# First stage of a two-layer graph and mixture-of-experts kernel on one core: two GpSimd roots of different groups in one instruction, eight scatters in a row behind it

## The reference

```python
x = x + gnn0(_layernorm(x), adj)        # adj @ (x @ w) + b
x = x + ffn0(_layernorm(x))             # attention over 64 nodes, then 8 experts, 2 per token
x = x + gnn1(_layernorm(x), adj)
x = x + ffn1(_layernorm(x))             # 6 experts, 2 per token
...
def _rmsnorm(v, w):
    return v * rsqrt(mean(v * v) + 1e-6) * w
# inside ffn0:
h = _rmsnorm(x, ln1_w)
...
x = x + y @ wo.T                        # y: softmax attention
flat = _rmsnorm(x, ln2_w)
probs = softmax(flat @ router_w.T)      # the two largest of 8 choose the experts
```

## Time and profile before

| what | us |
|---|---|
| time, median of 3 runs | 855.92 |
| the three runs | 860.66, 855.92, 854.97 |
| the profiled execution | 854.43 |
| its span, first to last instruction | 852.5 |
| busy PE / PEld / DVE / ACT / POOL | 811.2 / 624.2 / 697.4 / 521.3 / 426.0 |

### The profile page before, as it was taken

One profiled execution on the slowest core, in us unless ns is written; L12 is line 12 of the kernel. 1 busy time (PEld: TensorE's weight loads), 2 busy tenths in 40 slices (PEclk: granted clock), 3 DMA queues, 4 the chain that ended last, 5 costly groups with the idle time before them and its releaser, 6 DMA issues.

```text
span 852.5 us, 21598 instructions
## 1 busy us (share of the span) xinstructions
PE 811.2 (95%) x6244; PEld 624.2 (73%) x6245; DVE 697.4 (82%) x2699; ACT 521.3 (61%) x1120; POOL 426.0 (50%) x413
## 2 busy tenths in 40 slices
PE   7998999999788899999999999899999999999997
PEld 7675777777547899999999999566665655555563
DVE  4899988989867798877777888888888888888863
ACT  3666787786645466556565654556566656655664
POOL 4248888888877300940100042566665566666300
PEclk9899999999999999999999999999999999999999
DMA  9602411131115766676666762344443344443323
GB/s 269 178 12 78 114 52 48 54 112 42 45 42 171 201 189 174 172 194 167 174 170 163 176 181 75 111 123 124 122 124 120 118 138 147 152 131 121 108 88 99
DMA packets 107591, 108.25 MB, mean 127 GB/s; under 512 B 27822, under 2 KB 89600, under 8 KB 105344
## 3 DMA queue, kind: packets, MB, share of 16 engines
q1 hardware_dynamic: 96976, 88.52, 36.4%
q0 software_dynamic: 8880, 18.19, 7.0%
q10 hardware_dynamic: 1664, 0.66, 0.3%
HBM read 82.07 MB, written 25.26 MB: 126 GB/s over the span
## 4 chain that ended last, share of the span: by engine, by line
PE 61%; issue 4%; POOL 3%; DVE 1%; DMA 1%; ACT 0%; SPq 0%; POOLq 0%; DVEq 0%
PE banks L2073 16%; PE banks L2113 10%; PE banks L2237 10%; PE banks L2229 9%; PE banks L2205 7%; PE banks L2088 2%; PE banks L2134 2%; PE banks L2145 1%; PE banks L2162 1%; PE banks L2251 1%; PE banks L2174 1%; POOL slots_in L1292 1%; POOL expert_rows L1352 1%; PE banks L2154 1%; DMA slots_out<-ys 0%
## 5 line engine op out<-in xcount | busy, mean ns | idle before, releaser
L1352 POOL DMA_INDIRECT expert_rows<-slots_out,slot_c x128 | 140.8, 1100 | 74.6 <-DVE ys L1610 42.1
L326 POOL DMA_INDIRECT slots_in<-flat,slot_now x115 | 120.7, 1050 | 35.7 <-issue 31.2
L2073 PE MATMUL banks<-xT_hi,w_hi 128*128 128x256 f32 (+1 forms) x426 | 127.0, 298 | 0.4 <-DVE w_lo L1629 0.4
L2073 PE MATMUL banks<-xT_hi,w_lo 128*128 128x256 f32 (+1 forms) x426 | 120.7, 283 | 0.0
L2073 PE MATMUL banks<-xT_lo,w_hi 128*128 128x256 f32 (+1 forms) x426 | 120.4, 283 | 0.0
L2113 PE MATMUL banks<-w_sb,prod 128*128 (+1 forms) x852 | 107.1, 275 | 2.4 <-DVE ys L1610 2.4
L2113 PEld LDWEIGHTS banks<-w_sb,prod 128*128 128x128 f32 (+1 forms) x852 | 101.3, 191 | 2.8 <-issue 2.6
L2073 PEld LDWEIGHTS banks<-xT_hi,w_hi 128*128 128x128 f32 (+1 forms) x426 | 76.2, 179 | 0.6 <-issue 0.6
L2073 PEld LDWEIGHTS banks<-xT_lo,w_hi 128*128 128x128 f32 (+1 forms) x426 | 76.6, 180 | 0.0
L2073 PEld LDWEIGHTS banks<-xT_hi,w_lo 128*128 128x128 f32 (+1 forms) x426 | 76.2, 179 | 0.0
L1426 ACT ACTIVATE w_hi<-w_raw 128x684 fp32r<-128x684 f32 x71 | 54.9, 773 | 26.3 <-PE banks L2073 26.3
(11 more groups left out here) (306 smaller groups left out, 2116.7 us busy)
## 6 DMA issues: line engine op xcount, KB each, us to landing
w_raw<-in_w SPq DMA_DIRECT2D x71, 342.0 KB, 3.4
f_all<-gates_dram SPq DMA_DIRECT2D x16, 1024.0 KB, 6.7
xs<-slots_in SPq DMA_DIRECT2D x71, 128.0 KB, 2.6
slots_out<-ys SPq DMA_DIRECT2D x71, 128.0 KB
f_all<-gates_dram SPq DMA_DIRECT2D x16, 512.0 KB, 4.5
base_all<-in_x SPq DMA_DIRECT2D x16, 256.0 KB, 4.2
out<-ob SPq DMA_DIRECT2D x16, 256.0 KB
slots_in<-zrow SPq DMA_DIRECT2D x20, 128.0 KB, 3.5
```

Of the source, the lines that this page charges most:

```text
L326: G.indirect_dma_start(out=slots_in, out_offset=bass.IndirectOffsetOnAxis(ap=slot_now0[g % 2][:, n:n + 1], axis=0), in_=flat[g % 2][:, n / ...
L1352: G.indirect_dma_start(out=rows[p][:, n, :], out_offset=None, in_=slots_out[0:filled(g) * R, :], in_offset=bass.IndirectOffsetOnAxis(ap=sl ...
L2073: last = T.matmul(banks[bank][0:m, half * R:(half + 1) * R], ww[:, par, n * HIDP + c * P:n * HIDP + c * P + m], xx[:, par, :], start=q == ...
```

## The change

For the groups 0 to 11 (`g < JOINT`, with `APART = 4`) the root of the sum of squares is no longer an instruction of its own. VectorE writes the mean of squares of group g as a third row of `var_b` beside the variances of group g + 4, and GpSimd's `rstd1(g + 4)` takes all three rows in one instruction of 128 x 12. It waits for both. The groups 12 to 15 keep their own root. The joint root and the eight scatters of a round now stand together: the root behind `ln_pow`, then 5, 1, 7 of one group and 0, 3, 6, 4, 2 of the next. On ScalarE `flat_` of these groups moves from behind `xn_` to a place between `exp` and `hp_` of its next round. On VectorE `var1` goes ahead of `yn_`. The pipeline gets one more (empty) round.

```diff
+            APART, JOINT = 4, NG - 4
-            var_b, rs_b = sb("var_b", [P, NG, 2, TG]), sb("rs_b", [P, NG, 2, TG])
+            var_b, rs_b = sb("var_b", [P, NG + APART, 3, TG]), sb("rs_b", [P, NG + APART, 3, TG])
...
-            DEEP = 7
+            DEEP = 8
...
                     def rstd1(g):
                         if g is not None:
+                            n = 2
                             pool.wait_ge(at["var1"], upto("var1", g + 1))
-                            G.tensor_tensor(rs_b[:, g, :, :], var_b[:, g, :, :], mhalf[:, 0:2 * TG].rearrange("p (k t) -> p k t", k=2), ALU.pow).then_inc(at["rstd1"], 1)
+                            if exists(g - APART):
+                                n = 3
+                                pool.wait_ge(at["ssv"], upto("ssv", g - APART + 1))
+                            G.tensor_tensor(rs_b[:, g, 0:n, :], var_b[:, g, 0:n, :], mhalf[:, 0:n * TG].rearrange("p (k t) -> p k t", k=n), ALU.pow).then_inc(at["rstd1"], 1)
...
                     def rms(g):
-                        if g is not None:
+                        if g is not None and g >= JOINT:
...
                     def body(g, new):
                         ln_pow(new)
-                        scatter(2, g[6])
+                        rstd1(g[1])
+                        if g[6] is None or g[6] >= JOINT:
+                            scatter(2, g[6])
                         scatter(5, g[6])
                         rms(g[5])
                         scatter(1, g[6])
                         scatter(7, g[6])
                         scatter(0, g[5])
-                        rstd1(g[1])
                         scatter(3, g[5])
                         scatter(6, g[5])
                         scatter(4, g[5])
+                        if g[5] is not None and g[5] < JOINT:
+                            scatter(2, g[5])
...
                     def flat_(g):
...
-                            act.wait_ge(at["rms"], upto("rms", g + 1))
+                            if g < JOINT:
+                                act.wait_ge(at["rstd1"], upto("rstd1", g + APART + 1))
+                            else:
+                                act.wait_ge(at["rms"], upto("rms", g - JOINT + 1))
...
                         exp(g[6])
+                        if g[8] is not None and g[8] < JOINT:
+                            flat_(g[8])
                         hp_(g[4])
...
                         xn_(g[2])
-                        flat_(g[7])
+                        if g[7] is not None and g[7] >= JOINT:
+                            flat_(g[7])
                         vd(g[5])
...
                         slotf(g[6])
                         mv1(g[2])
                         slot(g[6])
+                        var1(g[2])
                         yn_(g[5])
-                        var1(g[2])
```

More of the change, by code:

```diff
@@ L170, in build @@
             st_b, mv_b = sb("st_b", [P, NG * TG, 6]), sb("mv_b", [P, NG * TG, 2])
-            var_b, rs_b = sb("var_b", [P, NG, 2, TG]), sb("rs_b", [P, NG, 2, TG])
+            var_b, rs_b = sb("var_b", [P, NG + APART, 3, TG]), sb("rs_b", [P, NG + APART, 3, TG])
             nmr, inv_h, ratio = (sb(n, [P, NG * TG]) for n in ("nmr", "inv_h", "ratio"))
-            ss, ssv = (sb(n, [P, NG * TG]) for n in ("ss", "ssv"))
+            ss = sb("ss", [P, NG * TG])
             mx, rden = sb("mx", [P, NH, TG]), sb("rden", [P, TG, NH])
@@ L309, in rstd1 @@
                         if g is not None:
+                            n = 2
                             pool.wait_ge(at["var1"], upto("var1", g + 1))
-                            G.tensor_tensor(rs_b[:, g, :, :], var_b[:, g, :, :], mhalf[:, 0:2 * TG].rearrange("p (k t) -> p k t", k=2), ALU.pow).then_inc(at["rstd1"], 1)
+                            if exists(g - APART):
+                                n = 3
+                                pool.wait_ge(at["ssv"], upto("ssv", g - APART + 1))
+                            G.tensor_tensor(rs_b[:, g, 0:n, :], var_b[:, g, 0:n, :], mhalf[:, 0:n * TG].rearrange("p (k t) -> p k t", k=n), ALU.pow).then_inc(at["rstd1"], 1)
                     def rms(g):
-                        if g is not None:
+                        if g is not None and g >= JOINT:
                             pool.wait_ge(at["ssv"], upto("ssv", g + 1))
-                            G.tensor_tensor(tiles(rr2, g), tiles(ssv, g), mhalf[:, 0:TG], ALU.pow).then_inc(at["rms"], 1)
+                            G.tensor_tensor(tiles(rr2, g), var_b[:, g + APART, 2, :], mhalf[:, 0:TG], ALU.pow).then_inc(at["rms"], 1)
                     def scatter(n, g):
@@ L440, in flat_ @@
                                 n = g * TG + t
-                                last = S.activation(flat[g % 2][:, t, :], f2_all[:, n, :], ACT.Copy, scale=rr2[:, n:n + 1])
+                                root = rs_b[:, g + APART, 2, t:t + 1] if g < JOINT else rr2[:, n:n + 1]
+                                last = S.activation(flat[g % 2][:, t, :], f2_all[:, n, :], ACT.Copy, scale=root)
                             last.then_inc(at["flat"], 1)
@@ L632, in ssv_ @@
                             dve.wait_ge(at["ssq"], upto("ssq", g + 1))
-                            V.tensor_scalar(tiles(ssv, g), tiles(ss, g), 1.0 / C, 1e-6, ALU.mult, ALU.add).then_inc(at["ssv"], 1)
+                            V.tensor_scalar(var_b[:, g + APART, 2, :], tiles(ss, g), 1.0 / C, 1e-6, ALU.mult, ALU.add).then_inc(at["ssv"], 1)
                     def lg_(g):
@@ L714, in scale_top @@
                         dve.wait_ge(at["dtop"], upto("dtop", g1))
-                        dve.wait_ge(at["rms"], upto("rms", g1))
-                        s = slice(g0 * TG, g1 * TG)
-                        V.tensor_tensor(top_all[:, s, :], top_all[:, s, :], rr2[:, s].unsqueeze(2).broadcast_to([P, (g1 - g0) * TG, 8]), ALU.mult).then_inc(dve_w, 1)
+                        if g1 <= JOINT:
+                            dve.wait_ge(at["rstd1"], upto("rstd1", g1 + APART))
+                            roots = rs_b[:, g0 + APART:g1 + APART, 2, :]
+                        else:
+                            dve.wait_ge(at["rms"], upto("rms", g1 - JOINT))
+                            roots = rr2[:, g0 * TG:g1 * TG].rearrange("p (g t) -> p g t", t=TG)
+                        scaled = top_all[:, g0 * TG:g1 * TG, :].rearrange("p (g t) e -> p g t e", t=TG)
+                        V.tensor_tensor(scaled, scaled, roots.unsqueeze(3).broadcast_to([P, g1 - g0, TG, 8]), ALU.mult).then_inc(dve_w, 1)
                     def body(g, new):
```

## The result

The changed kernel takes 865.29 us (median of five runs, 865.12 to 867.87) against 855.92 before: a ratio of 1.0122 with a 95% interval from 1.01 to 1.0143. It is slower by 1.2%. Its profiled execution has a span of 863.4 us against 852.5, 10.9 us more.

A forecast was written before the change was run, and what follows sets the result against it. GpSimd was taken to set the round. Being 16.3 us late at 104.07, with 3.9 recovered in later rounds of 13.07 us, gave +12.5 us on 855.92: forecast 868, range 864 to 873.

The forecast's parts named there:

- The price at the start: First two batches: `ln_pow` behind joint root and scatters, which wait for `flat`; 16.3 us late at 104.07.
- The new round is 2.50 + 10.00 + 0.57 = 13.07 us: Steady round on GpSimd: joint root, eight scatters, one scatter lengthened by `qk_rot`; 0.41 us less than 13.48.
- TensorE's 12.72 holds: Steady rounds: if no addition met a scatter, TensorE's busy time is the floor; 3.5 us less over ten rounds, +9.0.
- Behind it both kernels have the same order: After group 12's root, foretold at 236.0 instead of 223.55, nothing further was added to the +12.5 us.
- Faster: Rival: the queue behind `ln_pow` has no price, twelve merged roots save 4.9 us, 851 us; chance 0.07.
- Half the price: Rival: only the first batch is late, since group 1's `flat` comes in time; +6.1, 862 us; chance 0.08.
- No saving later: Rival: the steady round stays at 13.48 us; +16.6, 872.5 us; chance 0.12.
- the change doesn't act: Rival: joint root waits so late for `var_b` that all moves back, or stage's end hides it; 856 us; chance 0.03.
- The page: Skill page's port sharing would let scatters hold `qk_rot`, up to 1.9 us more; a trace row decided: nothing added.

The follow-up runs named there:

- ln_early: The changed kernel with each input batch's root `rs_a` moved on GpSimd from behind the round's scatters to ahead of scatter(0): 855.42 us, ratio 0.9979 to the kernel before.
- both_early: The changed kernel with `rs_a` ahead of scatter(0) and group 12's root behind scatter(3) of the round ahead: 855.82 us, ratio 1.0 to the kernel before.
- early_nmr_down: `both_early` with VectorE's use of the variances' root (`nmr`, `inv_h`) moved behind `topi`: 852.76 us, ratio 0.9949 to the kernel before.
- root12_early: The changed kernel with group 12's root of the sum of squares moved on GpSimd into the round ahead, behind scatter(3): 864.42 us, ratio 1.009.
- flat_first: The changed kernel with `flat` on ScalarE ahead of the exponential instead of behind it, `rs_a` left in place: 858.79 us, ratio 1.0026 to the kernel before.

## Why the prediction was right, and where its sizes were off

Forecast 868.0 us (864 to 873), slower with 0.82; measured 865.29, slower. The mechanism and its place were right, and two terms had the wrong size.

*The price at the start: right.* The chain that was written down comes out at each link: first scatter foretold at 69.8 (68.77), `rs_a` at 76.1 and 97.7 (75.10 and 97.15), `nm_a` standing 7.3 and 6.4 us (7.21 and 6.71), GpSimd idle for 4.1 us twice (4.18 twice), group 6's root at 104.07 (103.65). The offset of 1 us is `pr`, which ran at 65.50 instead of 66.50. In all the start was 15.9 us late (103.65 against 87.72). `ln_early` then showed that 13.5 of them hang on the place of `ln_pow`; the other 2.4 go with the first scatters, which wait for `flat` in both kernels (68.77 and 68.27).

*"The new round is 2.50 + 10.00 + 0.57 = 13.07 us": the step that was mis-sized.* 2.50 + 10.00 held to 0.02 us. The 0.57 us weren't there. The step rested on "VectorE reaches `qk_rot` a fixed time behind `nmr`, which waits for `rs_b`", and it stops holding when VectorE doesn't wait for `rs_b`. Where it does wait, in `ln_early` and `both_early`, the round is 13.09 us: the term's arithmetic was good, its condition unchecked. From group 6's root to that of group 12 the sum had 131.9 us, and it took 127.8 (one round of 13.87 with the one scatter that was held, eight of 12.52, then 13.8): 4.1 us less. The root of group 12 came 7.9 us late in place of 12.5.

*"TensorE's 12.72 holds": wrong as a floor.* The busy time of TensorE in a slower round isn't its need. In the changed kernel it is 115.45 / 117.00 of 12.52, or 12.35 us a round, and `early_nmr_down` runs at 12.50. Part of what counts as busy in a slower round is waiting inside groups of matmuls: the 64 matmuls of the scores take 1.37 to 1.42 us in eight rounds of the kernel before (1.37 at 130.04) and 0.91 or 0.92 in each steady round of the changed one (0.91 at 128.72), at a clock of 1.00 in both. That bound allowed 3.5 us less over ten rounds where 5.7 (ten times 0.57) were to be had, though the measured time stayed in the range.

*"Behind it both kernels have the same order": true, and no reason for the same time.* The separate root of group 12 stands behind a full row of the scatters that used to be spread around it, and the passage cost 2.8 us. `root12_early` gave 2.75 back.

The misses have opposite signs: 0.4 and 4.1 us too much, 2.8 us too little. Without the one the forecast would have been about 863.5, without the other 871. So the time's place inside the range is in part luck: had the passage cost nothing, as the sum had it, the measured 865.29 would have been about 862.5, below the range.

*The rivals.* "Faster" named its condition rightly: `rs_a` before 68.8 and 84.0. `ln_early` meets it (63.91, 80.94), and even so comes out at 855.42 and not 851. With `rs_a` in time the scatters still begin late for `flat` (68.27 for 61.09), group 6's joint root is 2.4 us behind the scatter of the earlier trace rows that it stands ahead of (90.17 for 87.72), ten rounds with the collision in them make of this 0.9 us ahead at the root of group 12 (222.66), and the passage to the separate roots turns it into 0.7 us behind at that of group 14 (247.27). "Half the price" was wrong: both batches paid. `flat_first` shows that half the price was to be had by the order on ScalarE. "No saving later" and "the change doesn't act" are out by the round of 12.52 us and the span.

*The page.* In the changed kernel `qk_rot` starts 0.18 to 0.22 us behind a scatter's start and takes 1.21 to 1.23 us, nine rounds long, and in `early_nmr_down` it starts 0.15 us behind. Nothing was to be added to the sum, as the row said. The Trainium skill ("SBUF — State Buffer", section "SBUF: two separate sides") would have whichever of the two starts first hold the other for its whole instruction, if the GpSimd operation reads SBUF. For this pair the traces show one direction only: a scatter holds no `qk_rot`, wherever in it the addition starts. Small operations of VectorE are another matter, as the last section shows; they are too short to be seen in the sum.

## What to carry to other kernels

Before an instruction is put behind another on an in-order queue, follow who waits for it, and whether the instruction ahead of it waits for the same engine in its turn: here one small root behind a row of scatters closed a circle, and moving it gave 13.5 us back. When a round shows a collision of fixed length, ask which wait holds the two engines in step. Taking that wait away can be worth as much as taking work away (0.57 us a round here), and moving the colliding instruction itself is riskier than it looks. And a merged instruction has an edge where merging starts or ends. Price that passage as well as the steady round.

## What the runs showed of the hardware that was not expected

A GpSimd instruction that starts while VectorE's `qk_rot` (1.22 us) adds two SBUF tensors is held until 1.10 us after that addition's start, and then takes its usual time. With d for the distance between the two starts, a scatter's duration here was 0.97 + 1.10 - d to 0.03 us: 1.94 at d = 0.13, 1.65 at 0.42, 1.55 at 0.53, 1.45 at 0.62, 1.16 at 0.91, 1.00 at 1.06; and 2.11 for a root of 1.05 at d = 0.03 (other roots fell up to 0.07 us short of the formula). A scatter that started ahead of the addition (by 0.03 to 0.96 us in the traces) kept its usual time and didn't lengthen the addition (1.21 to 1.23 us). So for this pair the whole cost of the meeting depends on who is first, and the difference is 1 us.

The other direction exists too, for small operations of VectorE. Many that started 0.5 us or more behind a scatter's start, and would have ended before it, ended together with it, to 0.01 us. The usual 0.17 us became 0.44 in `early_nmr_down`, where the scatter of 141.34 ends at 142.31:

```profile
141.86 0.44 DVE L654 TENSOR_SCALAR var_b<-ss 128x4 f32<-128x4 f32 x1 [0.27 <-ACT junk L444]
```

The operation behind it started at its usual distance all the same. Of those that started in a scatter's first 0.45 us none was held. Why some are and others not, the traces don't show.

TensorE's wait of 5.95 us at 235.93 cost more than its length: the eight projections behind it took 5.46 us in place of 3.60, at a granted clock that averages 0.89 over that stretch.
